# A fused attention and memory-lookup block: the part behind attention written out in a new order

## The reference

```python
x = x + _layernorm(_L0_attn_ref(_layernorm(x, axis=-1), ...), axis=-1)   # 16 heads of 16, softmax attention, projection
x = x + _layernorm(_L0_ffn_ref(_layernorm(x, axis=-1), ...), axis=-1)

# _L0_ffn_ref, RD = 48, BOT = 128, N = 1024, K = 8
query = jnp.einsum('bsh,dh->bsd', hidden_states, q_proj_w)
rq = jnp.einsum('bsd,rd->bsr', query, router_w)
rk = jnp.einsum('nd,rd->nr', aux_keys, router_w)
scores = jnp.einsum('bsr,nr->bsn', rq, rk) / math.sqrt(RD)
scores = scores + reliability_mask[None, None, :]
top_scores, top_idx = jax.lax.top_k(scores, K)
log_var = jnp.log1p(variance)                      # of hidden_states, per row
normalized_var = log_var / (log_var.mean() + 1e-06)   # mean over all 4096 rows
h1 = jax.nn.gelu(jnp.einsum('bsh,fh->bsf', hidden_states, unc_w1) + unc_b1, approximate=False)
learned = (jnp.einsum('bsf,of->bso', h1, unc_w2) + unc_b2)[..., 0]
uncertainty = jnp.clip(normalized_var * 0.5 + jax.nn.sigmoid(learned) * 2.5, 0.0, 5.0)
gate = jax.nn.sigmoid(gate_w1 * uncertainty + gate_bias)
w = jax.nn.softmax(top_scores, axis=-1)
agg = jnp.einsum('bsk,bskh->bsh', w, aux_values[top_idx])
out = hidden_states + gate[..., None] * agg
```

## Time and profile before

| | us |
|---|---|
| median of 3 runs (3212.37 to 3213.76) | 3212.43 |
| profiled execution, its own time | 3212.74 |
| its span, first to last instruction | 3210.7 |
| PE busy in the span | 3098.2 (96%) |
| DVE busy | 2834.2 (88%) |
| ACT busy | 2504.5 (78%) |
| POOL busy | 262.0 (8%) |

### The profile page before, as it was taken

How to read it: one execution, slowest core, us unless ns; L and a number is a source line. 1 busy time by engine, 2 the same in 40 slices (tenths; PEclk the granted TensorE clock), 3 DMA queues, 4 the chain that set the end, 5 groups by cost and what they waited for, 6 DMA issues and landing times.

```text
span 3210.7 us, 70961 instructions
## 1 busy us (share of the span) xinstructions
PE 3098.2 (96%) x26983; PEld 1357.5 (42%) x26983; DVE 2834.2 (88%) x3108; ACT 2504.5 (78%) x4551; POOL 262.0 (8%) x810
## 2 busy tenths in 40 slices
PE   8999999999999999999999999999999999998883
PEld 4544444444444444344444334444444434465652
DVE  5599999999999999999999999999999999356666
ACT  5288888888888888888888888888888888733333
POOL 2400000000000000000000000000000000101103
PEclk9799999999999999999999999999999999989996
DMA  7320202010101010101010101011010110000001
GB/s 255 59 41 1 41 1 41 1 41 2 41 1 37 5 34 8 34 8 31 11 27 14 24 18 24 18 21 21 18 24 14 27 30 1 1 0 0 0 0 52
DMA packets 27354, 82.72 MB, mean 26 GB/s; under 512 B 4641, under 2 KB 15633, under 8 KB 24018
## 3 DMA queue, kind: packets, MB, share of 16 engines
q1 hardware_dynamic: 26818, 77.84, 10.5%
q0 software_dynamic: 272, 1.05, 0.1%
HBM read 57.90 MB, written 20.97 MB: 25 GB/s over the span
## 4 chain that ended last, share of the span: by engine, by line
PE 94%; DVE 2%; issue 1%; ACT 1%; POOL 0%; DVEq 0%; POOLq 0%; ACTq 0%
PE ps L1022 41%; PE ps L1031 36%; PE ps L1235 4%; PE ps L998 3%; PE ps L957 2%; PE ps L1184 2%; PE ps L1041 1%; PE ps L1224 1%; PE ps L1159 1%; PE ps L971 1%; PE ps L1049 1%; PE ps L949 1%; DVE partial L750 1%; ACT q_raw L619 0%; PE ps L1201 0%
## 5 line engine op out<-in xcount | busy, mean ns | idle before, releaser
L750 DVE TENSOR_REDUCE partial<-ps 128x1 f32<-128x1024 f32 x2048 | 2482.4, 1223 | 123.7 <-PE ps L998 101.7
L577 ACT ACTIVATE work<-ps 128x512 f32<-128x512 f32 x4096 | 2207.6, 596 | 344.7 <-PE ps L1022 136.6
L998 PE MATMUL ps<-k_stack,q_stack 48*128 48x512 f32 x4096 | 1532.6, 453 | 4.9 <-DVE partial L750 4.2
L1022 PE MATMUL ps<-q_stack,k_stack 64*128 64x512 f32 x4096 | 1510.2, 448 | 0.5 <-ACT work L577 0.5
L1031 PE MATMUL ps<-work,v_head 128*32 128x256 f32 x16384 | 1296.1, 391 | 0.0
L1022 PEld LDWEIGHTS ps<-q_stack,k_stack 64*128 64x128 f32 x4096 | 632.2, 184 | 807.6 <-ACT work L577 676.5
L998 PEld LDWEIGHTS ps<-k_stack,q_stack 48*128 48x128 f32 x4096 | 634.3, 187 | 46.1 <-DVE partial L750 40.8
L1031 PEld LDWEIGHTS ps<-work,v_head 128*32 128x32 f32 x16384 | 329.1, 108 | 697.2 <-ACT work L577 581.5
L423 POOL CAST nm_parts<-negmax 128x4 bf16<-128x4 f32 x128 | 25.0, 195 | 2272.6 <-DVE negmax L757 2272.6
L1235 PE MATMUL ps<-k_raw,q_raw 128*128 128x256 f32 x512 | 127.6, 406 | 17.8 <-ACT q_raw L619 17.8
L619 ACT ACTIVATE q_raw<-ps 128x1024 f32<-128x1024 f32 x32 | 32.8, 1025 | 132.6 <-PE ps L1224 132.6
(11 more groups left out here) (128 smaller groups left out, 1074.4 us busy)
## 6 DMA issues: line engine op xcount, KB each, us to landing
k_stack<-qk_parts SPq DMA_DIRECT2D x96, 256.0 KB, 4.1
q_stack<-qk_parts SPq DMA_DIRECT2D x96, 256.0 KB, 4.1
qk_parts<-qk_part SPq DMA_DIRECT2D x32, 512.0 KB, 2.8
x_sb<-L_attn_x SPq DMA_DIRECT2D x8, 512.0 KB, 10.8
out<-work SPq DMA_DIRECT2D x8, 512.0 KB, 2.9
k_raw<-L_ffn_aux_values SPq DMA_DIRECT2D x1, 1024.0 KB
work<-L_attn_w_qkv POOLq DMA_DIRECT2D x1, 768.0 KB, 7.3
q_raw<-L_ffn_aux_keys SPq DMA_DIRECT2D x1, 512.0 KB
```

Of the source, the lines that this page charges most:

```text
L577: act.activation(probs[:, g % DEPTH, a, :], ps[:, bank, :], ACT.Exp, scale=SCALE).then_inc(exp_done, 1)
L750: dve.tensor_reduce(partial[:, k // 4, k % 4:k % 4 + 1], ps[:, 2 * slot:2 * slot + 2, :], AX.XY, ALU.max).then_inc(max_used, 1)
L998: last = pe.matmul(ps[:, 2 * slot + e, :], q_stack[HALF:HALF + ROWS, b1, c * CH + (k // 4) * P:c * CH + (k // 4 + 1) * P], k_stack[HALF:HA ...
L1022: pe.matmul(ps[:, bank, :], k_stack[0:HALF, b, P * g:P * (g + 1)], q_stack[0:HALF, b, at:at + CH], start=True, stop=True).then_inc(s_ready, 1)
```

## The change

Every list behind attention is written out anew, and with it the steps put into it = 63.

- The product of `q_proj_w` and `router_w` is made once (`route_weights`), and stands beside the hidden layer's weights in `wcat`. One pair of 512-column matmuls per chunk (R, `route`) gives `ru`: rows 0 to 47 the routing query, rows 64 to 127 the hidden layer; ACT moves both with one instruction that adds the bias, in which row 48 is the constant for the reliability mask. query, hidden layer and rq of before are gone.
- DVE's combination writes `attn` by rows, so PE transposes it as it is. `stage_a`, `stage_h` and their copies are gone. DVE's attention loop has a head, four iterations, to a pass, 15 passes (31 passes of two iterations before).
- The variance of the normalised rows is worked out on POOL from the numbers it has (`normed_variance`); `norm_stats` is gone.
- There are two wT buffers, and one bank for A. S runs two tiles ahead throughout; Y and aT run two and three chunks ahead, H and R one.
- In it = 63 PE gets aT for three chunks, Y for two, and H and R of chunk 0; before it had aT for two and Y for one.
- The gate of chunks 0 to 6 is worked out in chunk 6, that of chunk 7 in chunk 7. The results, normalisations and additions are spread over chunks 6 and 7.

The core of the diff:

```diff
-        attn = sb("attn", [P, NC * TPC * C + 8 * D])
+        attn = sb("attn", [P, NT * C])
...
+        hT = work[:, 5120:6144].rearrange("p (k t) -> p k t", k=CC)
+        ru = work[:, 6144:6656]
+        g1T = k_raw[:, 2048:2560]
...
+        wcat = q_raw[:, 6400:6656].rearrange("p (k n) -> p k n", k=CC)
...
+        wT_flat = [q_raw[:, 1024 * b:1024 * (b + 1)] for b in range(2)]
+        wT = [v.rearrange("p (v t) -> p v t", v=NV) for v in wT_flat]
+        wT2 = [v.rearrange("p (a n) -> p a n", a=2) for v in wT_flat]
+        attn_rows = attn[:, :].rearrange("p (t c) -> p t c", c=C)
+        attn_pairs = attn[:, :].rearrange("p (q a i h d) -> p q h i a d", q=PAIRS, a=4, i=2, h=H)
...
+            def normed_variance(c):
+                pool.wait_ge(rs_ready, c * 2 + 2)
+                pool.tensor_tensor(veps[:, :], rstd[:, :], rstd[:, :], ALU.mult).then_inc(hv_own, 1)
+                pool.wait_ge(hv_own, c + 1)
+                pool.tensor_tensor(hvar[:, TPC * c:TPC * (c + 1)], veps[:, :], mv[:, :, 1], ALU.mult).then_inc(hv_done, 1)
+            for c in range(NC):
                 block_powers(c)
-                stage_attn(c + 2)
...
-                block_powers(c)
...
+            def move_ru(c):
+                act.wait_ge(r_psum, c + 1)
+                act.activation(ru, ps[:, 3, :], ACT.Identity, bias=rbias).then_inc(r_ready, 1)
...
+            attend(ITS - 1, None, {11: lambda: move_aT(0), 17: lambda: move_aT(1), 23: lambda: move_aT(2),
+                                   28: lambda: move_hT(0), KG - 1: lambda: move_ru(0)})
...
+            def gelu(c):
+                if c > 0:
+                    act.wait_ge(l_psum, c)
+                act.wait_ge(r_ready, c + 1)
+                act.activation(g1T[RUS:RUS + F1, :], ru[RUS:RUS + F1, :], ACT.Gelu).then_inc(u_ready, 1)
...
+            gelu(0)
+            exponentials(0)
+            move_hT(1)
+            exponentials(1)
+            for c in range(NC - 2):
+                n = c * TPC
+                move_wT(n)
+                exponentials(n + 2)
+                if c > 0:
+                    move_hT(c + 1)
+                move_wT(n + 1)
+                move_ru(c + 1)
+                if c + 3 < NC:
+                    move_aT(c + 3)
+                exponentials(n + 3)
+                gelu(c + 1)
+                move_wT(n + 2)
+                exponentials(n + 4)
+                move_wT(n + 3)
+                exponentials(n + 5)
+            n = (NC - 2) * TPC
...
+            n = (NC - 2) * TPC
+            log_variance()
+            gate_exp((0, n + TPC, learned), l_ready, NC - 1)
+            move_wT(n)
+            exponentials(n + 2)
+            move_hT(NC - 1)
+            move_wT(n + 1)
+            move_ru(NC - 1)
+            exponentials(n + 3)
+            gate_exp((0, n + TPC, gate), g_a, 1)
+            gelu(NC - 1)
+            move_wT(n + 2)
+            exponentials(n + 4)
+            move_wT(n + 3)
+            exponentials(n + 5)
+            n = (NC - 1) * TPC
+            gate_exp((n, NT, learned), l_ready, NC)
+            move_wT(n)
+            exponentials(n + 2)
+            normalise(0)
+            move_wT(n + 1)
+            exponentials(n + 3)
+            gate_exp((n, NT, gate), g_a, 2)
+            normalise(1)
+            move_wT(n + 2)
+            normalise(2)
+            move_wT(n + 3)
+            for c in range(3, NC):
+                normalise(c)
...
-                dve.tensor_tensor(attn[:, bass.ds(it * (8 * D), 8 * D)].rearrange("p (a i d) -> p i a d", a=4, i=2),
+                dve.tensor_tensor(attn_pairs[:, pair, bass.ds(h, 1), :, :, :].rearrange("p o i a d -> p (o i) a d"),
...
+            row_max(AHEAD, range(LEAD, LEAD + 32), 0, 0, PAIRS - 1, H - 1)
+            with dve.Fori(0, H - 1) as h:
+                for j in range(PAIRS):
+                    row_max(h * (2 * PAIRS) + (2 * j + 2 + AHEAD), range(LEAD, LEAD + 32), h * PAIRS + (j + 1), (j + 1) % 2, j, h)
...
+            def result(c):
+                b = c % 4
+                if c >= 4:
+                    dve.wait_ge(res_ready, c - 3)
+                dve.wait_ge(agg_ready, TPC * (c + 1))
+                for i in range(TPC):
+                    n = c * TPC + i
+                    last = dve.scalar_tensor_tensor(out=o2[b][:, i, :], in0=attn_rows[:, n, :], scalar=gate[:, n:n + 1],
+                                                    in1=h_tile(c, i), op0=ALU.mult, op1=ALU.add)
+                last.then_inc(o_own, 1)
+                dve.wait_ge(o_own, 3 * c + 1)
+                tile_stats(lambda i: o2[b][:, i, :], 3 * c + 1, o_own, o_mv[:, b, :, :]).then_inc(o_own, 1)
+                dve.wait_ge(o_own, 3 * c + 3)
...
+            for c in range(1, NC - 2):
+                n, ahead = c * TPC, c + 2
+                keep_agg(n - 1)
+                weigh(n + 1)
+                projected(ahead, 0)
+                take_top(n + 2)
+                keep_agg(n)
+                projected(ahead, 1)
+                weigh(n + 2)
+                projected_stats(ahead)
+                take_top(n + 3)
+                keep_agg(n + 1)
+                add_block(ahead)
+                weigh(n + 3)
+                block_stats(ahead)
+                take_top(n + 4)
+                keep_agg(n + 2)
+                norm_block(ahead)
+                weigh(n + 4)
+                keep_learned(c + 1)
+                take_top(n + 5)
...
+            n = (NC - 2) * TPC
+            keep_agg(n - 1)
+            weigh(n + 1)
             dve.wait_ge(lv_ready, 1)
             dve.reduce_sum(lvs, lv, axis=AX.X).then_inc(lv_own, 1)
...
+            take_top(n + 2)
+            mean_log()
+            keep_agg(n)
+            weigh(n + 2)
+            gate_argument(0, n + TPC, 2, 0)
+            take_top(n + 3)
+            keep_agg(n + 1)
+            weigh(n + 3)
+            gate_value(0, n + TPC, 6, 0)
+            take_top(n + 4)
+            result(0)
+            keep_agg(n + 2)
+            weigh(n + 4)
+            keep_learned(NC - 1)
+            take_top(n + 5)
+            result(1)
+            n = (NC - 1) * TPC
+            keep_agg(n - 1)
+            weigh(n + 1)
+            gate_argument(n, NT, 8, 1)
+            take_top(n + 2)
+            result(2)
+            keep_agg(n)
+            weigh(n + 2)
+            take_top(n + 3)
+            gate_value(n, NT, 12, 1)
+            result(3)
+            keep_agg(n + 1)
+            weigh(n + 3)
+            result(4)
+            result(5)
+            keep_agg(n + 2)
+            result(6)
+            keep_agg(n + 3)
+            result(7)
...
+                for k in range(CC):
+                    last = pe.matmul(ps[:, 2, 2 * P + HALF * k:2 * P + HALF * k + RD], qpw[:, P * k:P * (k + 1)], routT,
+                                     start=True, stop=True)
                 last.then_inc(w3_t, 1)
...
+            def route(c, free, n):
+                pe.wait_ge(free, n)
+                pe.wait_ge(hT_ready, c + 1)
+                for k in range(CC):
+                    last = pe.matmul(ps[:, 3, :], wcat[:, k, :], hT[:, k, :], start=(k == 0), stop=(k == CC - 1))
+                last.then_inc(r_psum, 1)
...
+            def aggregate(n):
+                pe.wait_ge(wT_ready, n + 1)
+                if n == 0:
+                    pe.wait_ge(l_ready, 1)
+                else:
+                    pe.wait_ge(agg_ready, n)
+                for v in range(NV):
+                    last = pe.matmul(ps[:, 2, 0:C], wT[n % 2][:, v, :], values[:, v, :],
+                                     start=(v == 0), stop=(v == NV - 1))
+                last.then_inc(agg_psum, 1)
...
+                   {2: transpose_weights, 6: route_weights,
+                    10: lambda: attn_transpose(0, w3_e, 4),
+                    13: lambda: project_out(0, 0, 2, w3_e, 5),
+                    14: lambda: project_out(0, 1, 3, comb_used, ITS + CREDIT[comb_used]),
+                    16: lambda: attn_transpose(1, aT_ready, 1),
+                    19: lambda: project_out(1, 0, 2, y_evac, 1),
+                    20: lambda: project_out(1, 1, 3, y_evac, 2),
+                    22: lambda: attn_transpose(2, aT_ready, 2),
+                    27: lambda: norm_transpose(0, aT_ready, 3),
+                    30: lambda: route(0, y_evac, 4)})
+            lookup_scores(0)
+            project_out(2, 0, 3, r_ready, 1)
...
+            learn(0, 2, y_evac, 3)
+            project_out(2, 1, 3, y_evac, 5)
+            pe.wait_ge(comb_used, ITS + 1 + CREDIT[comb_used])
+            lookup_scores(1)
+            norm_transpose(1, hT_ready, 1)
+            transpose_picked(0, hT_ready, 2)
+            lookup_scores(2)
+            aggregate(0)
+            transpose_picked(1, wT_ready, 1)
+            lookup_scores(3)
+            route(1, y_evac, 6)
+            attn_transpose(3, wT_ready, 2)
+            aggregate(1)
+            transpose_picked(2, aT_ready, 4)
+            lookup_scores(4)
```

(54 more changed lines are left out.)

555 lines of the change are left out of this document (215 added, 340 removed).

## The result

The changed kernel takes 3170.61 us (median of four runs, 3168.35 to 3175.9) beside 3212.66 of the kernel before on the same chip: ratio 0.9871, 95% interval 0.9854 to 0.9888. It is faster, but the forecast was 3118 and the range ended at 3152: of the 94 us that were to be saved, 42 came. The profiled execution took 3175.9 with a span of 3174.0, 5.3 above the median; the forecast of the span was 3116.2. All times here are medians of runs in the faster of the two states that this chip shows, which leaves out one single run, of after_padded, with 3861.97 us at a granted clock of 0.65.

What follows compares the result with a forecast made beforehand. TensorE's clock is full nearly throughout; behind attention, chunks of 44.42 us held 34.9 of PE work, the rest clock and waits. +10.5 - 62.3 - 42.7 = -94.5 gave span 3116.2, forecast 3118 us, range 3103 to 3152.

Steps and rivals of the forecast that it cites:

- Attention itself: Attention's iterations: the combination's new write and the longer DVE loop add no time; iterations stay at 41.07 us.
- DVE's loop must fetch its code: Rival, chance 0.10: each of 15 jumps back in DVE's attention loop waits 2.9 to 4.1 us, +44 to +61.
- an edge costs nothing now: Argument on DVE's attention loop before the change: spans with and without a loop's edge differ by only 0.03 us.
- Steady chunks: Chunks 1 to 5: 32.15 us of PE work plus one wait of 2.0 before A(n+3), 34.1 each, 170 together.
- A at 3.46: Chunks 1 to 5: every A takes 3.46 us at full clock and never 4.5, also behind the wait.
- the clock keeps falling: Rival, chance 0.12: PE's clock still falls beside waits, 3.6 us in each of seven chunks, +25, 3143 us.
- Chunk 0: From attention's end: 37.1 us of PE work plus 5.5 of waits, 42.6 together.
- it = 63: Attention's last iteration: inserted work on PE and ACT adds 10.5 us, 49.0 becoming 59.5.
- Chunks 6, 7 and the end: DVE sets the pace, last result at 78 us, then 10.6 to the end; taken as 90 for 132.7, minus 42.7.
- DVE nearly without pause in all of the last 75 us: Expected sign at the kernel's end: DVE busy nearly without pause in the last 75 us.
- Longer wait loops: Rival, chance 0.09: a second wait of 3 us in each chunk with its knock-on, 3135 to 3150 us.
- a slower kernel: Rival, chance 0.03: attention's 62 pieces with a combination each grow by more than 1.5 us; at 2 us, 3242.

Runs made afterwards that it cites:

- after_padded: The changed kernel with 120 semaphore increments that nothing waits for, put ahead of DVE's attention loop: 3176.35 us, ratio 0.9897.
- after_written_out: The changed kernel with DVE's attention loop (15 passes of four iterations) written out, no backward jump left: 3126.23 us, ratio 0.9732.
- swapped kernel: after_written_out with ACT's move of wT(n+3) put ahead of exp(n+4) in chunks 0 to 5: 3118.52 us, ratio 0.9713.

## Why the prediction was wrong

**Attention itself, "Cost nil": this step failed, by 41.5 us.** The sum took the edge of DVE's loop as free because it was free in the kernel before. The rival *DVE's loop must fetch its code* had the place, the mechanism and nearly the price (2.9 to 4.1 for each of 15 jumps, +44 to +61; DVE stands still for 2.8, and the time lost is 3.0 over 14, +41.5), and 0.10 was too little for it. That the time lost is so near the stall is luck: it is PE's wait of 1.3 to 1.55 us and, in ten of the 14, the clock, which the rival did not price. The rival's count was good (312 instructions estimated, 306 compiled), but it was argued from size, and against size alone the runs speak: the same body costs nothing 40 instructions earlier. What decided is where the body begins, and the change moved that by writing one iteration out ahead of the loop. No row of before shows such a stall; but the rival's bounds came out of rows, and 0.10 was all that the argument "an edge costs nothing now" was worth against them.

**Steady chunks: the wait was right, the clock was not.** PE work without the wait, the wait's place, its cause and its size (2.0 forecast, 1.70 to 2.02 measured) hold; a chunk at full clock takes 34.43 for 34.1. The failed term is "A at 3.46" behind the wait: 6.6 to 6.8. That is the rival *the clock keeps falling* (0.12), whose price of 3.6 a chunk, read from T, S and A of the kernel before, is near the 3.1 that an A of 6.6 to 6.8 loses; the argument against it, that the wait has S before and A behind, was no protection. S and T were mis-sized by 0.28 for each of four tiles, since their price was that of 65 rows, and one L of 1.05 went for nothing beside S: net +0.1, two errors that cancel. Together +15.3.

**Chunk 0: 42.6 forecast, 47.9 measured.** A(2) at 6.28, behind L and its wait of 1.96 for Gelu, is 2.8 of it, again the clock; the rest is that L (1.70 for 1.05), the same S and small waits.

**it = 63: 59.5 forecast, 58.1 measured.** Right, the list of inserted work on PE and ACT priced row by row.

**Chunks 6, 7 and the end: 90 forecast, 87.2 measured.** Right, with the mechanism: in the changed kernel the chain that ended last runs from 3107 to 3164 nearly all on DVE's rows, with DVE busy 48.7 of 53 us, and the last result stands at 3160.16, its statistics done at 3163.9, 77 us behind the start for the 78 that were forecast. DVE nearly without pause in all of the last 75 us was too much said: it was busy 57.1 of them, since the last ten are POOL's and the transfer's. The first A of chunk 6 waits 0.55 and not 3; in after_written_out it waits 0.84, and in the swapped kernel, where PE comes 11.4 us earlier than there, 4.28.

Longer wait loops and a slower kernel did not come. The forecast's chance for faster, 0.95, was sound; what failed was a sum that put nil on a loop that it had itself found a reason to doubt.
